# The multiply of the tile one-hots in `route` goes from VectorE to GpSimd

## The reference

```python
x = x + _L0_xattn_ref(_layernorm(x, axis=-1), ctx_1024, ctx_1024, ...)
x = x + _L0_ffn_ref(_layernorm(x, axis=-1), L0_ffn_Wr, L0_ffn_W1, L0_ffn_W2)
...
x = x + _L3_xattn_ref(_layernorm(x, axis=-1), ctx_1024, mask_BxS2_bk0, ...)
x = x + _L3_ffn_ref(_layernorm(x, axis=-1), L3_ffn_rw1, ...)
return x
```

```python
router_probs = jax.nn.softmax(router_logits, axis=-1)
top_p, top_i = jax.lax.top_k(router_probs, TOP_K)
top_p = top_p / top_p.sum(axis=-1, keepdims=True)
h = jax.nn.gelu(jnp.einsum('bsd,edh->bseh', x, w1) + b1, approximate=False)
expert_out = jnp.einsum('bseh,ehd->bsed', h, w2) + b2
sel = jnp.take_along_axis(expert_out, top_i[..., None], axis=2)
return (top_p[..., None] * sel).sum(axis=2)
```

## Time and profile before

| | us |
|---|---|
| median of 3 runs | 1701.83 |
| lowest and highest | 1696.3 and 1709.65 |
| the profiled execution | 1709.13 |
| its span in the trace | 1707.4 |

### The profile page before, as it was taken

One profiled execution on the slowest core, in us unless ns is written; L12 is line 12 of the kernel. 1 busy time (PEld: TensorE's weight loads), 2 busy tenths in 40 slices (PEclk: granted clock), 3 DMA queues, 4 the chain that ended last, 5 costly groups with the idle time before them and its releaser, 6 DMA issues. The chain is left out here.

```text
span 1707.4 us, 30271 instructions
## 1 busy us (share of the span) xinstructions
PE 1152.6 (68%) x8662; PEld 912.2 (53%) x8664; DVE 795.3 (47%) x2048; ACT 619.5 (36%) x1225; POOL 846.6 (50%) x950
## 2 busy tenths in 40 slices
PE   3547744892766766626757789947999785777771
PEld 2437643682566766515434455524788534676661
DVE  4540007457732222278883432335799526222223
ACT  2124436341344444344321122214445531444443
POOL 6136647464145555543445768845344102555553
PEclk9668976996889888968987999978899896888896
DMA  3051125000411111120312445540000013111114
GB/s 105 2 165 40 40 76 104 4 0 7 161 32 39 38 38 40 36 99 13 91 50 50 93 89 98 113 75 10 1 0 0 7 61 117 38 40 40 37 40 159
DMA packets 87545, 95.95 MB, mean 56 GB/s; under 512 B 19605, under 2 KB 66838, under 8 KB 86966
## 3 DMA queue, kind: packets, MB, share of 16 engines
q1 hardware_dynamic: 63974, 59.90, 11.8%
q0 software_dynamic: 23040, 33.06, 8.7%
q10 hardware_dynamic: 464, 2.16, 0.3%
HBM read 65.72 MB, written 29.36 MB: 56 GB/s over the span
## 5 line engine op out<-in xcount | busy, mean ns | idle before, releaser
L974 PE MATMUL psum<-f_xsT,f_w1e 128*128 128x128 f32 x1472 | 234.5, 310 | 164.4 <-issue 111.6
L974 PEld LDWEIGHTS psum<-f_xsT,f_w1e 128*128 128x128 f32 x1472 | 210.5, 220 | 180.7 <-issue 149.4
L945 POOL DMA_INDIRECT d_y<-f_y,f_dst x184 | 181.2, 985 | 199.4 <-DVE f_y L1068 137.4
L941 POOL DMA_INDIRECT f_xs<-d_xn,f_src x184 | 178.2, 969 | 144.9 <-SPq L937 89.7
L1053 DVE TENSOR_TENSOR f_hpre<-psum,f_b 128x512 f32<-128x512 f32 x144 | 99.6, 692 | 264.5 <-remote 98.3
L982 PE MATMUL psum<-f_w,f_hT 128*128 x1472 | 217.2, 296 | 1.0 <-ACT f_hT L1023 0.6
L982 PEld LDWEIGHTS psum<-f_w,f_hT 128*128 128x128 f32 x1472 | 202.0, 213 | 1.8 <-issue 1.8
L481 PE MATMUL psum<-ident,xn 128*128 128x128 f32 x256 | 48.5, 370 | 172.5 <-DVE xn L454 172.3
L1008 ACT COPY f_w1e<-f_w 128x512 f32 x184 | 113.7, 618 | 70.1 <-PEq L1658 32.6
L481 PEld LDWEIGHTS psum<-ident,xn 128*128 128x128 f32 x256 | 41.8, 193 | 178.3 <-ACT xn L495 174.1
L1023 ACT ACTIVATE f_hT<-f_hpre 128x512 f32<-128x512 f32 x144 | 90.7, 630 | 109.5 <-DVE f_hpre L1053 89.8
(11 more groups left out here) (461 smaller groups left out, 2359.6 us busy)
## 6 DMA issues: line engine op xcount, KB each, us to landing
f_yback<-d_y SPq DMA_DIRECT2D x20, 512.0 KB, 6.6
d_xn<-xn SPq DMA_DIRECT2D x3, 2048.0 KB, 7.6
f_w<-in_L_ffn_W SPq DMA_DIRECT2D x2, 2048.0 KB, 13.7
a_v<-in_ctx SPq DMA_DIRECT2D x4, 1024.0 KB, 8.5
f_wg<-in_WgT SPq DMA_DIRECT2D x16, 256.0 KB
f_wu<-in_WuT SPq DMA_DIRECT2D x16, 256.0 KB
f_wd<-in_WdT SPq DMA_DIRECT2D x16, 256.0 KB
f_xs<-d_xn,f_src POOLq DMA_INDIRECT x184
```

Of the source, the lines that this page charges most:

```text
L941: nc.gpsimd.indirect_dma_start(xs[:, u % RX, :], None, k.d_xn, bass.IndirectOffsetOnAxis(m.src[:, n:n + 1], 0)).then_inc(gathered[u % RX], 16)
L945: nc.gpsimd.indirect_dma_start(k.d_y, bass.IndirectOffsetOnAxis(m.dst[:, n:n + 1], 0), y[:, u % RT, :], None).then_inc(scattered[u % RT], 16)
L974: last = nc.tensor.matmul(BH[u % 2][:, s * P:(s + 1) * P], w1e[:, u % RT, s * P:(s + 1) * P], xsT[:, u % 2, :], start=True, stop=True)
```

## The change

GpSimd makes `ohi`. VectorE makes `picked` and `ohr` of a group, and signals the first by `tile_hot` and the second by a new semaphore, `row_hot`. GpSimd has a loop of its own behind the tables: for each group it waits for `picked` and for the matmuls that last read this buffer of `ohi`, and multiplies. TensorE waits for `row_hot` and for `oh`. VectorE no longer waits for its own one-hots.

```diff
--- before.py
+++ after.py
@@ -764,8 +764,8 @@
         steps, exd, rk, oh = [k.sem(f"{tag}_{s}") for s in (
             "dve_steps", "exp_done", "ranked", "onehots")]
         xst, wl, one_used = [k.sem(f"{tag}_{s}") for s in ("xn_stored", "weights_loaded", "onehots_used")]
-        tile_hot, tables, late = [k.sem(f"{tag}_{s}") for s in (
-            "tile_onehots", "tables_made", "late_steps")]
+        tile_hot, row_hot, tables, late = [k.sem(f"{tag}_{s}") for s in (
+            "tile_onehots", "row_onehots", "tables_made", "late_steps")]
         m.weights_loaded = wl
         count = {}
         with nc.Block() as block:
@@ -839,9 +839,7 @@
                     js = slice(g * GR, (g + 1) * GR)
                     wait(dve, one_used, g - 1)
                     TT(picked[:, g % 2], col_of[:], bc(fii[:, js], (P, m.cols, GR), 1), ALU.is_equal).then_inc(tile_hot, 1)
-                    TT(ohr[:, g % 2], row_of[:], bc(fri[:, js], (P, P, GR), 1), ALU.is_equal).then_inc(tile_hot, 1)
-                    dve.wait_ge(tile_hot, 2 * g + 2)
-                    TT(ohi[:, g % 2], picked[:, g % 2], bc(tokv[:, js], (P, m.cols, GR), 1), ALU.mult).then_inc(oh, 1)
+                    TT(ohr[:, g % 2], row_of[:], bc(fri[:, js], (P, P, GR), 1), ALU.is_equal).then_inc(row_hot, 1)
                 step = Steps(dve, late)
                 step(TT(cmp_[0:1], bc(k.iota_f[0:1, 0:m.cols], (1, m.cols, NE), 2), bc(cumt[0:1], (1, m.cols, NE), 1), ALU.is_ge))
                 step(RED(ef[0:1], cmp_[0:1], AX.X, ALU.add))
@@ -871,6 +869,12 @@
                 nc.gpsimd.tensor_copy(tokv[:], k.tokval[:]).then_inc(tables, 1)
                 if beside is not None:
                     beside.pool(pool)
+                pool.wait_ge(tables, 3)
+                for g in range(NG):
+                    pool.wait_ge(tile_hot, g + 1)
+                    wait(pool, one_used, g - 1)
+                    nc.gpsimd.tensor_tensor(ohi[:, g % 2], picked[:, g % 2], bc(tokv[:, g * GR:(g + 1) * GR], (P, m.cols, GR), 1),
+                                            ALU.mult).then_inc(oh, 1)
 
             @block.scalar
             def _(act):
@@ -891,6 +895,7 @@
                 if beside is not None:
                     beside.tensor_middle(pe)
                 for g in range(NG):
+                    pe.wait_ge(row_hot, g + 1)
                     pe.wait_ge(oh, g + 1)
                     for u in range(GR):
                         at = g * GR + u
```

## The result

The changed kernel takes 1707.37 us (median of 20 runs, 1695.88 to 1712.22), the kernel before 1701.82 us (20 runs beside them). The ratio is 1.0032, with a 95% interval of 1.0018 to 1.0046: 5.5 us slower, between 3.1 and 7.8. It is less than the 1% of the prediction's bounds, and with twenty runs a side its sign is nevertheless plain.

What follows compares the result with a forecast made beforehand. VectorE paces f3 and TensorE f1, and delays of `jj` pass on one for one. f3 +5.4, f1 +1.5 and f0 +1.1 make +8.0 us, so the median 1701.83 becomes 1709.8 us, range 1700 to 1721.

Steps and rivals of the forecast that it cites:

- turns: In the three loops GpSimd and VectorE alternate on SBUF inputs: 2.14 us a group in f3, +8.0 us overall; chance 0.78.
- Whole instructions: Each engine holds the shared pair for a full instruction: 2.54 us a group in f3, +16.0 us in all.
- so I take the first line: GpSimd's multiply priced from fp32 rows with two full inputs: 1.40 us at 72 columns, 0.86 at 40.
- low bound: GpSimd's multiply priced from operations with a repeated column: 1.15 us for 576 elements, 0.72 for 320.
- high bound: GpSimd's multiply at double the price, since bf16 may need an unpacking pass; no row for it.
- the low price: Turns with GpSimd's multiply at the low bound: 1.89 us a group in f3, +4.3 us in all, 1706.1 us.
- The comparison at the end: After f3's loop, L846 queues behind GpSimd's last multiply and five steps follow: `jj` at 19.65 against 14.25, +5.4 us.
- f1's sum in the prediction: In f1 `jj` comes at 475.25 against 473.75, +1.5 us; TensorE's own pace of 2.0 us hides the rest.
- What the changed profile would show: In f3 `ohi` 1.8 to 2.0 us, starts 2.1 apart, `picked` well above 1 us, `ohr` near 685 ns.
- Side by side: In the three loops bf16 operations do not collide: sum -2.5 us, 1699.3 us; chance 0.09.
- The dear multiply: GpSimd's bf16 multiply takes 2.8 us for 576 elements, 3.55 us a group: +33.8 us, 1735.6 us; chance 0.11.
- rival 2: Engines run without colliding: f3's `jj` after 12.8 us (-1.45), sum -2.5 us, 1699.3 us; chance 0.09.

Runs made afterwards that it cites:

- price run: Kernel before, plus GpSimd products of scratch tiles in f3's router block, fp32 and bf16, full or repeated second input; executed once, 1560 us.
- the iota: Kernel before, plus on GpSimd for each group an iota that reads nothing and writes an unread scratch tile; 1561.78 against 1560.65 us, ratio 1.0007.
- the numbers in PSUM: Kernel before with tile and row numbers copied into PSUM, so `picked` and `ohr` read one input there; multiply still on VectorE; 1559.61 us, ratio 1.0000.
- The third buffer: Changed kernel with three buffers instead of two for `picked`, `ohr` and `ohi`; 1561.02 against 1558.24 us for the kernel before, ratio 1.0020.
- the reads experiment: Kernel before, plus on GpSimd for each group an unread product of the same size with both inputs in SBUF; 1568.28 against 1560.65 us, ratio 1.0052.
- the combination: Changed kernel with tile and row numbers in PSUM and three buffers; 1553.97 against 1558.24 us for the kernel before, ratio 0.9971; repeated on another chip, 0.9984.
- the late steps: The combination with VectorE's five steps from the comparison to `padsrc` put between the groups; 1562.94 against 1558.24 us for the kernel before, ratio 1.0021.

## Why the prediction was right

*The mechanism, turns: right.* The prediction set a group to three turns, 0.326 + 0.555 + 1.263 us. The trace shows the three as 0.31, 0.60 and 1.01. That they are turns is shown from both sides: reads added to the kernel before stretch VectorE, writes don't, and with one input out of SBUF the move costs f3 0.4 us instead of 3.4. Whole instructions one behind another would be 0.456 + 0.685 + 1.148 = 2.29 us a group; at 1.92 the trace is again shorter than the whole-instruction hold that the prediction took from the Trainium skill, "SBUF — State Buffer", section "Who interferes with whom", by 0.12 us a turn.

*The price of GpSimd's multiply: mis-sized.* The step "so I take the first line" gave 1.40 us at 72 columns. It measured 1.15 (and 0.72 at 40), the prediction's own low bound. That the two agree is luck: the low bound was drawn from fp32 operations with a repeated column, and that form measured 1.19. The fp32 line is right for fp32; the operation is bf16 with an operand repeated along the outer axis, which is cheaper. Nor did bf16 need more time, for which the high bound doubled the price: 1.274 us against 1.408. This one term explains most of the error: with the low price the prediction gives 1.89 us a group, 17.6 us for f3 and +3.3, +0.5 and +0.5 us, measured 1.92, 17.63, +3.38, +0.57 and +0.66 (f1's +0.5 stands there without a working, since by the turns alone f1 would end before TensorE's pace lets it). The sum was forecast as +8.0 us (+4.3 with the low price), measured +4.6 in the profile and +5.5 between medians. The +8.0 lies just above the interval's 7.8, and the measured time lies well inside the range because the range allows some 10 us either way; the change itself was forecast too large.

*The comparison at the end: right.* GpSimd's last multiply goes ahead of it (1.69 us), and the five steps come behind. *f1: right in kind*, TensorE's pace hides most; the prediction had `jj` wait for VectorE's end, +1.5 us, and measured is a later first group of TensorE, +0.57. That size holds only at one clock. Over the stretch from the first `picked` to `jj` f1 takes 18.17 us at a mean granted clock of 0.82 in the kernel before and in the price run, 19.33 at 0.79 in the repeat of the changed kernel, 19.79 at 0.70 beside the iota, and 20.77 at 0.64 with the numbers in PSUM, where VectorE's work was not stretched at all. In all of them the stretch begins at the lower level (0.50, 1.2 GHz), after TensorE had idled, and ends at the higher (1.00, 2.4 GHz). In the price run the window from 440 to 445 us is already at 1.00, with the numbers in PSUM it is still at 0.50. So f1 differs by up to 2.6 us with TensorE's clock, for which f1's sum in the prediction has no term. In the repeat the three places are 3.38 + 1.16 + 0.66 = 5.2 us.

*What the changed profile would show: half right.* The multiply lasts 1.53 us and not 1.8 to 2.0, by the price. `picked` was to be "well above 1 us": with two buffers it is in f3 only the second, at 1.40; the others wait for TensorE during the same hold and then show 0.8. The third buffer makes them all 1.40 at the same pace. `ohr` keeps 679 ns, as forecast.

*The rivals.* Side by side is refuted by the stretched rows and by the reads experiment. The dear multiply is refuted by 1148 ns. f3 does become shorter than before, as rival 2 forecast (12.8 us), but only where VectorE's one-hots read one input from PSUM and there is a third buffer (11.6 us).

*Left open:* the 0.9 us between 4.6 and 5.5, which the interval covers, the half microsecond ahead of the gather in the combination, and some 3 us of the combination's gain and of the loss with the late steps.

## What to carry to other kernels

Before an element-wise operation is moved from VectorE to GpSimd, look at what VectorE does meanwhile: if both read SBUF and VectorE has two inputs there, the two took turns in this kernel, and the group cost the sum of both (1.92 us a group instead of 1.47), with the dearer engine's price in it. The mark of it in a timeline is ends that follow one another although starts overlap, and durations that change with the neighbour. If one of VectorE's inputs is small and used over and over, try a copy of it in PSUM: here it removed the collision at the same rate (`picked` 1.40 to 0.45 us). Check then which buffer ring becomes the bound, and keep other small VectorE steps out of that stretch. And where TensorE sets the pace, read its granted clock before a difference of a microsecond is put down to the change.

## What the runs showed of the hardware

- VectorE's bf16 compare with one input from PSUM runs as fast as with both from SBUF (454 against 456 ns at 576 elements, 0.68 us at 1024).
- GpSimd's multiply of 576 elements takes 1408 ns in fp32, 1274 in bf16, 1148 in bf16 with an operand that repeats along the outer axis; an fp32 one gains nothing from that repeat and 0.22 us from a repeat along the inner axis (1186).
- GpSimd's multiply with inputs in SBUF and VectorE's operations with two inputs there take turns, each turn 0.08 to 0.15 us shorter than the operation alone (0.31 us for `picked`, 0.60 for `ohr`, 1.01 for the multiply). Beside an iota of GpSimd, which only writes, VectorE's multiply stays at 458 ns, and a reduction of VectorE stays at 0.73 us beside GpSimd's multiply.
- The same kernel takes 9% longer on one chip than on another. The experts' first matmuls in the kernel before (1702 us) and in the price run (1560 us), with busy us, mean ns and idle time before:

```profile
L974 PE MATMUL psum<-f_xsT,f_w1e 128*128 128x128 f32 x1472 | 234.5, 310 | 164.4 <-issue 111.6 <-ACT f_xsT L1013 44.3 <-ACT f_w1e L1008 8.0
```

```profile
L974 PE MATMUL psum<-f_xsT,f_w1e 128*128 128x128 f32 x1472 | 212.1, 289 | 51.6 <-issue 28.9 <-ACT f_xsT L1013 13.7 <-ACT f_w1e L1008 7.0
```

  Of the 150 us between them, 113 are idle time of TensorE ahead of this one line, and 83 of these are put down to issue. Why one chip issues these more slowly no run here tells.
